# Writing the input gates' rows straight to their partitions, with new slot tables: an xLSTM, attention and expert kernel on one core

## What is computed

```python
igate = gate_input @ ig_kernel + ig_bias         # (8, 512, 4)
fgate = gate_input @ fg_kernel + fg_bias
cums = cumsum(log_sigmoid(fg))                   # F
log_D = cums[t] - cums[s] + ig[s]                # t >= s, else -inf
D = exp(log_D - max_log_D)                       # max over s
C = (q k^T / sqrt(64)) * D
h = (C / (max(|sum C|, exp(-max_log_D)) + eps)) @ v
x = x + headnorm(h)
...
q, k, v = per mixture m and head, of layernorm(x)
attn = softmax(q k^T / 4)                        # 2 x 16 heads, 512 x 512 per batch
x = x + sum_m probs_m * (attn v) wo_m
x = x + sum over the best 2 experts of p_k * (gelu(n2 fw1_k) fw2_k)
```

## Time and profile before

| | |
|---|---|
| median of 3 runs | 1423.28 us (1422.08 to 1424.86) |
| profiled execution | 1428.74 us |
| its span | 1426.9 us |
| PE busy | 1393.6 us, 98% |
| DVE, ACT, POOL busy | 77%, 64%, 25% |
| mean granted clock of PE | 0.99 of full speed |

### The profile page before, as it was taken

One profiled execution on the slowest core, in us unless ns is written; L12 is line 12 of the kernel. 1 busy time (PEld: TensorE's weight loads), 2 busy tenths in 40 slices (PEclk: granted clock), 3 DMA queues, 4 the chain that ended last, 5 costly groups with the idle time before them and its releaser, 6 DMA issues.

```text
span 1426.9 us, 22218 instructions
## 1 busy us (share of the span) xinstructions
PE 1393.6 (98%) x7666; PEld 716.9 (50%) x7666; DVE 1092.2 (77%) x2299; ACT 916.4 (64%) x1706; POOL 363.6 (25%) x351
## 2 busy tenths in 40 slices
PE   8999899999999999999999999999999999999999
PEld 5643434455454654555445554455545454454456
DVE  5779977987789877987779877797769986786721
ACT  3266557766677666675677765876666766757752
POOL 6512342203313123132241133130331322330000
PEclk9999999999999999999999999999999999999999
DMA  4056037430854127441464308541084413561002
GB/s 116 17 70 95 2 45 107 71 62 16 104 76 76 45 38 112 75 75 31 51 101 69 64 31 101 79 75 46 24 102 70 78 56 45 73 77 46 17 1 89
DMA packets 92308, 90.15 MB, mean 63 GB/s; under 512 B 16483, under 2 KB 87267, under 8 KB 91295
## 3 DMA queue, kind: packets, MB, share of 16 engines
q1 hardware_dynamic: 92196, 88.73, 38.6%
HBM read 35.05 MB, written 4.25 MB: 28 GB/s over the span
## 4 chain that ended last, share of the span: by engine, by line
PE 69%; issue 8%; DVE 4%; DMA 3%; SPq 2%; POOL 1%; ACT 1%; DVEq 0%; POOLq 0%; ACTq 0%
PE psum L881 12%; PE psum L866 12%; PE psum L851 12%; PE psum L819 7%; PE psum L838 6%; PE psum L701 5%; PE psum L452 5%; PE psum L736 3%; DMA qst<-mrow 3%; PE psum L475 2%; SPq L1954 2%; PE psum L563 2%; DVE mx L1378 1%; PE psum L573 1%; DVE x L1293 1%
## 5 line engine op out<-in xcount | busy, mean ns | idle before, releaser
L1378 DVE TENSOR_REDUCE mx<-psum 128x1 f32<-128x512 f32 x1024 | 645.5, 681 | 134.2 <-PE psum L851 133.5
L1677 ACT ACTIVATE prob<-psum 128x512 f32<-128x512 f32 x1024 | 568.2, 600 | 270.8 <-PE psum L881 159.4
L866 PE MATMUL psum<-qst,kst 98*128 98x512 bf16 x1024 | 355.9, 383 | 10.5 <-DMA qst<-mrow 8.7
L851 PE MATMUL psum<-kst,qst 96*128 96x512 bf16 x1024 | 318.8, 381 | 2.9 <-DVE resid L1252 1.3
L881 PE MATMUL psum<-prob,vst 128*17 128x512 f32 x2048 | 248.1, 601 | 2.7 <-ACT prob L1677 2.3
L866 PEld LDWEIGHTS psum<-qst,kst 98*128 98x128 bf16 x1024 | 96.9, 99 | 220.8 <-issue 126.9
L851 PEld LDWEIGHTS psum<-kst,qst 96*128 96x128 bf16 x1024 | 99.0, 98 | 121.2 <-issue 17.9
L881 PEld LDWEIGHTS psum<-prob,vst 128*17 128x17 f32 x2048 | 46.7, 97 | 136.3 <-issue 106.8
L838 PE MATMUL psum<-w,cxT 128*128 128x256 f32 x448 | 105.4, 381 | 0.0
L819 PE MATMUL psum<-n2T,x 128*128 128x512 f32 x224 | 103.0, 592 | 0.0
L1828 POOL CAST parts<-resid 128x512 bf16<-128x512 f32 x64 | 41.0, 640 | 239.9 <-DVE resid L1252 239.9
(11 more groups left out here) (244 smaller groups left out, 1761.5 us busy)
## 6 DMA issues: line engine op xcount, KB each, us to landing
kst<-parts SPq DMA_DIRECT2D x186, 128.0 KB, 4.7
qst<-parts SPq DMA_DIRECT2D x186, 128.0 KB, 5.9
cmat<-G_dram SPq DMA_DIRECT2D x7, 1024.0 KB, 4.6
x<-in_L_ffn_fw SPq DMA_DIRECT2D x14, 512.0 KB, 3.7
w<-in_L_ffn_fw SPq DMA_DIRECT2D x14, 512.0 KB, 4.2
xbuf<-in_x SPq DMA_DIRECT2D x8, 512.0 KB, 5.1
kin<-in_ctx SPq DMA_DIRECT2D x8, 512.0 KB, 4.5
out<-acc SPq DMA_DIRECT2D x7, 512.0 KB, 9.0
```

Source lines behind the costliest of these rows:

```text
L851: e.matmul(psum[:, u.bank, :], qst[0:KROWS, h, t * P:(t + 1) * P], kst[0:KROWS, h, :], start=True, stop=True).then_inc(u.full, 1)
L866: e.matmul(psum[:, u.bank, :], kst[0:KROWS + 2, h, g * P:(g + 1) * P], qst[0:KROWS + 2, h, :], start=True, stop=True).then_inc(u.full, 1)
L1378: e.tensor_reduce(mx[:, qq * QUAD + j, t:t + 1], psum[:, u.bank, :], AX, ALU.max).then_inc(u.free, 1)
L1677: e.activation(prob[:, g % 2, j, :], psum[:, u.bank, :], ACT.Exp).then_inc(u.free, 1)
```

## The change

ScalarE writes the input gates of PSUM rows 32 to 35 to partitions 0 to 3 of `cmat` itself. The eight transfers of SyncE go, and VectorE's step g waits for ScalarE's release of the PSUM bank. `load_x(1)` waits for the statistics of batch 0, which that transfer's place had covered. All slot tables and the `AHEAD` strings are new; three numbers that place steps beside them are too (`SENT` 0: `send_rows` stands one slot nearer to its maxima in SyncE's program; `MADE` 125 for 118: GpSimd's making of the expert input `x3`, L1875 and L1879, stands seven slots later; `COPY` 2 for 3). The diff, with SyncE's part of the `MIDDLE` table standing for all tables:

```diff
@@ -158,7 +158,6 @@
         gi, gf, ga, lf = (cmat[0:NH, r, :] for r in range(4))
-        gi_made = cmat[GI:GI + NH, 0, :]
@@ -290,86 +289,86 @@
-        CARRY, MADE = 9, 118
-        VALUES, COPY, TURN = 1, 3, 7
-        LATER, SENT = 1, 1
+        CARRY, MADE = 9, 125
+        VALUES, COPY, TURN = 1, 2, 7
+        LATER, SENT = 1, 0
...
         MIDDLE = dict(
...
-            SP_A=slots(5, "ctx:0 x:9 gi G:65 s0:16 s1:2 s2:23 s3"),
-            SP_C=slots(47, "w10:5 w20:9 w11:10 w21:30 out"),
-            SP_S=slots(7, "s4:5 s5:15 s6:15 s7"),
+            SP_A=slots(3, "ctx:2 x:16 G:65 s0:7 s1:22 s2:0 s3"),
+            SP_C=slots(47, "w10:8 w20:11 w11:6 w21:34 out"),
+            SP_S=slots(6, "s4:0 s5:19 s6:9 s7"),
...
@@ -990,7 +989,7 @@
                 yield "g"
-                e.wait_ge(gi_moved, 16 * (b + 1))
+                e.wait_ge(uses["gates", b].free, uses["gates", b].n)
                 e.wait_ge(*va.at("F", b))
                 e.tensor_tensor(rows[:, 0, :], gi, gf, ALU.subtract).then_inc(va.here("g", b), 1)
@@ -1495,7 +1494,7 @@
                 yield "grow0"
-                e.activation(gi_made, psum[GI:GI + NH, u.bank, :], ACT.Identity, bias=gbias[GI:GI + NH, :]).then_inc(u.free, 1)
+                e.activation(gi, psum[GI:GI + NH, u.bank, :], ACT.Identity, bias=gbias[GI:GI + NH, :]).then_inc(u.free, 1)
@@ -1962,6 +1961,8 @@
             def load_x(b):
+                if b == 1:
+                    e.wait_ge(*va.at("stat", 0))
                 if b > 2:
                     e.wait_ge(*pc.at("acc0", b - 3))
@@ -1973,10 +1974,6 @@
                 yield "x"
                 if b > 1:
                     load_x(b)
-                yield "gi"
-                u = uses["gates", b]
-                e.wait_ge(u.free, u.n)
-                e.dma_start(gi, gi_made).then_inc(gi_moved, 16)
                 yield "G"
```

More of the change, by code:

```diff
@@ L311, in build @@
[L311 to L321, removed]
@@ new lines, in build @@
+            ACT_C={},
+            ACT_S=slots(0, "p3:0 pv0:3 pv1:2 p4:2 p5:12 p6:2 p7:7 v0:16 v1"),
+            POOL_A=slots(-8, "pw:17 vcopy:19 mask0:12 mask1:0 mask2:26 mask3:4 vw:0 hw:5 hs:16 hn:15 x2:4 r1:0 r5 s0:5 "
+                         "s1:5 s2:2 s3"),
+            POOL_C={},
+            POOL_S=slots(7, "s3:10 s4:6 s5:15 s6:16 s7"),
+            SP_A=slots(-8, "ctx:4 x:24 G:53 s0:15 s1:20 s2:11 s3"),
+            SP_C={},
+            SP_S=slots(2, "s3:5 s4:10 s5:14 s6:22 s7"),
+            AHEAD="4043031012001321221113202113314000011203110030410000001310101001"
+                  "0211021003000002000033020200221102300110120123000011020102000000")
@@ L351, in build @@
         LAST = dict(
             PE_A={},
-            PE_C=slots(5, "cxT00:3 cxT01:2 cxT10 cxT11:2 wo0 wo1 wo2:3 wo3:22 mean:7 n2T0:0 n2T1:3 logits:9 hid00 "
-                       "hid01:0 hid02:0 hid03 eo00:8 eo01 eo02:6 eo03:2 hid10:51 hid11:2 hid12:0 hid13:0 eo10:2 "
-                       "eo11:0 eo12:0 eo13"),
-            PE_S=slots(5, "p4:2 p5:15 p6:2 p7:5 v0:8 v1"),
+            PE_C=slots(5, "cxT00:2 cxT01:3 cxT10:2 cxT11:2 wo0:8 wo1:4 wo2:2 wo3 mean:18 n2T0:0 n2T1:6 logits:7 "
+                       "hid00:0 hid01:0 hid02:2 hid03:2 eo00:0 eo01:5 eo02:8 eo03 hid10:51 hid11:2 hid12:0 hid13:0 "
+                       "eo10:2 eo11:0 eo12:0 eo13"),
@@ L357, in build @@
+            PE_S=slots(3, "p4:0 p5:18 p6:3 p7:6 v0:0 v1"),
             DVE_A={},
-            DVE_C=slots(13, "wo0 wo1 wo2:3 wo3:4 bn0 bn1:0 bn2:6 bn3:0 var:9 n20:5 n21:0 n22:0 n23:5 mean:2 logits "
-                        "topk:11 acc00:6 acc01:5 acc02:4 acc03:56 acc10:0 acc11:0 acc12:0 acc13"),
-            DVE_S=slots(5, "s4:4 s5:14 s6 s7"),
+            DVE_C=slots(14, "wo0:8 wo1:4 wo2:2 wo3:3 bn0:0 bn1:0 bn2:0 bn3:0 var:8 n20:0 n21:0 n22:0 n23:10 mean:2 "
+                        "logits:3 topk:9 acc00:4 acc01:2 acc02:5 acc03:59 acc10:0 acc11:0 acc12:0 acc13"),
@@ L365, in build @@
             POOL_A={},
-            POOL_C=slots(7, "acc0:47 r1"),
-            POOL_S=slots(5, "s4:0 s5:10 s6:13 s7"),
+            POOL_C=slots(27, "acc0:32 r1"),
+            POOL_S=slots(6, "s4:4 s5:10 s6:25 s7"),
             SP_A={},
-            SP_C=slots(47, "w10:10 w20:11 w11:16 w21:51 out"),
-            SP_S=slots(12, "s4:2 s5:14 s6:9 s7"),
-            AHEAD="4102131020121223412100210103000310113001021000030102110000341104"
-                  "0100313000310031212400100220120001120001203102000021210000101000")
+            SP_C=slots(43, "w10:0 w20:17 w11:21 w21:53 out"),
@@ L373, in build @@
+            SP_S=slots(3, "s4:17 s5:9 s6:0 s7"),
+            AHEAD="4141011211011111301212140140114010110020001210111120001104101313"
+                  "0200031010100041213020002120111002111104120000120000200100002020")
         for plan in (FIRST, MIDDLE, LAST):
```

69 lines of the change are left out of this document (35 added, 34 removed), and 12 rows, old and new, of the table DVE_A.

## The result

The changed kernel takes 1431.83 us (1431.05 to 1432.18, 5 runs) against 1423.28 (1422.08 to 1426.18, 5 runs): 1.0056 times as long, 95% interval 1.0043 to 1.0069, or 8 us slower. The forecast was 1419.6 and faster.

What follows compares the result with a forecast made beforehand. PE was taken as the bound, busy 1393.6 of 1426.9 us. 1.1 us (head) plus 2.6 us (slot 96) made 3.7 us off the 1423.28 us median, giving 1419.6 us, range 1415.0 to 1427.

Steps and rivals of the forecast that it cites:

- The head: Before the first period: without the gates' transfer, step g starts 1.09 us earlier; 1.1 us gain counted in full.
- Slot 96: Middle periods: two more scores and maxima before PE's wait for the row transfer shorten it by 0.44 us, six times: 2.6 us.
- Slot 0: Middle periods' end: send for next quad 0, queued behind s2, store and s3, taken as in time; bound 4 us loss.
- Period 0: Batch 0's period: its 2.93 us wait at slot 96 stays, other waits move by tenths; nothing counted, 1 us either way.
- A wait for `mx` or `prob` where more maxima stand together: Sign of being wrong: a new PE wait for these in slots where more maxima now stand together; no size given.
- The middle periods apart from slot 96: Six middle periods: slot 96 taken as each one's only wait, PE work staying at 166.1 us; nothing else counted.
- everything else equal: Middle periods, p0 to slot 96: PE's work changes only from 14 scores and maxima to 16.
- The last period: Last period: expert weight loads stand in other slots; nothing counted, one wait of 0.95 us kept as the bound.
- The sum against one profile: Whole kernel: 3.7 us taken off the median; batch 3's extra 2.6 us could explain half the profile's 5.46 us excess.
- only the head moves: Rival: slot-96 waits stay, giving 1422.2 us; chance 0.31, shared with a gain partly eaten by slot 0.
- the first score of a period waits: Slower rival: at a period's end the send for quad 0 lands late, 1.8 us six times, giving 1430.4; chance 0.17.
- the larger gain: Rival: period 0's new order makes up for its 2.93 us wait and no half clock follows, giving 1415.0; chance 0.09.

Runs made afterwards that it cites:

- e1: Kernel before with all its tables and numbers, only the direct write added (no transfer of the gates): 1421.57 us, 0.9996 of before.
- e3: Changed kernel with period 0's whole table (FIRST) of before: 1427.01 us, 1.0029 of before.
- e8: Changed kernel, period 0's five maxima of slots 58 to 65 moved to slots 68, 70 and 71: 1431.55 us, 1.0060 of before.
- e13b: Changed kernel with period 0's GpSimd and SyncE rows of before: 1432.22 us, 1.0054 of before.
- e0: The kernel before, unedited, profiled a second time: 1423.44 us, span 1421.6.
- e2: Changed kernel with the middle periods' whole table of before: 1430.33 us, 1.0051 of before.
- e5: Changed kernel, middle table: VectorE's variance in slot 3 instead of 5, third and fourth query normalisations in slot 9 instead of 6: 1440.72 us, 1.0126 of before.
- e9: Changed kernel, middle table: eight transpositions of the attention's output on TensorE and ScalarE in slot 10 instead of 12: 1440.01 us, 1.0119 of before.
- e12b: Changed kernel, middle table: VectorE's statistics in slot 2, variance in 3, normalisations in 5, instead of 3, 5 and 6: 1433.60 us, 1.0069 of before.
- e16: Changed kernel, middle table: maxima of the first 16 slots placed as before: 1440.17 us, 1.0116 of before.
- e6: Changed kernel, last table: VectorE's four normalisations (L1292) in slot 43 instead of 39: 1432.55 us, 1.0061 of before.
- e14b: Changed kernel, last table: VectorE's four normalisations (L1292) in slot 42 instead of 39: 1432.33 us, 1.0061 of before.
- e7: Changed kernel with the edits of e5 and e6, and period 0's normaliser in slot 63 instead of 60: 1440.75 us, 1.0114 of before.
- e10: Changed kernel with the edit of e9 and the first and last tables of before: 1434.63 us, 1.0078 of before.

## Why the prediction was wrong

The sum was 1.1 for the head and 2.6 for slot 96; the result was a loss of 8. The step that failed is the one that put the rest of the new tables at nothing: period 0, the last period, and the middle periods apart from slot 96. Before's table alone gave back 3.8, 1.1 and 0.7 us there.

- **The head, 1.1 us.** The mechanism was right: e1 and the changed kernel's head show it. The size came from an execution whose transfer was issued late; in the second profile the wait is 0.46 us at step g and 0.60 at PE, and e1 wins 0.6 us of head. The 1.4 us by which the two shown profiles differ at L660 is not what the median saw.
- **Slot 96, 2.6 us.** The mechanism was right, the size somewhat too large. In the changed kernel the waits of L865 on the row transfers are 5.7 us; without period 0's 3.3 the other six hold 2.4 us, where the six at slot 96 held 4.2. So 1.8 us came of the 2.6. Five of the six shrank by 0.3 to 0.55 us, as worked out; the one in batch 3's period grew from 0.62 to 0.95. It is 0.94 to 1.52 us in every profile with the new middle table, edited or not, and 0.52 to 0.92 with the old one. Why is open.
- **Slot 0, counted at nothing with a bound of 4 us.** Right in value; no wait. The queue's end was put 2 to 3.5 us too late, 1.8 of it because I kept quad 7's send at its old time.
- **Period 0, "nothing counted, 1 us either way kept".** The largest single part of what failed. With the old table, 3.8 us come back (e3). I compared its order only at p0 and slot 96. PE's idle time there rises from 9.5 to 10.6 us over the old table's profiles to 11.6 to 12.2, and its clock column from 1.7 or 3.4 us to 3.4 to 6.8, mostly 5.1. As its cause, e8 and e13b exclude five maxima of slots 58 to 65 and the order of GpSimd and SyncE. The most conspicuous new row is a wait of 1.43 us for ScalarE's `prob`, behind a load of its tables (1.28 us), but it is not the loss. With the old table PE waits as long near there, under other names. The changed kernel, then e3:

```profile
99.32 0.28 PE L451 MATMUL psum<-ident,mx 128*16 128x128 f32 x1 [1.43 <-ACT prob L1676]
```

```profile
95.97 0.38 PE L851 MATMUL psum<-kst,qst 96*128 96x512 bf16 x1 [1.27 <-DVE resid L1252]
...
104.39 0.39 PE L866 MATMUL psum<-qst,kst 98*128 98x512 bf16 x1 [0.64 <-DMA qst<-mrow]
```

With a wait of 0.66 us at 95.6 in the changed kernel that is 2.1 against 1.9 us, and the seventeenth score starts at 104.52 against 104.39. The new idle time is elsewhere: 1.0 us in the next eight slots (four waits of 0.2 to 0.4 us between 106 and 114 us, three of them for maxima), 1.0 us between slots 64 and 72 (4.1 against 3.1 in e0 and e1), and 0.3 us at slot 96 (3.29 against 2.93 to 2.98). A wait for `mx` or `prob` where more maxima stand together was on the prediction's list of signs of being wrong; it had no price there. Which moves cause these waits stays open.
- **The middle periods apart from slot 96, counted at nothing.** I said that "everything else equal" holds between p0 and slot 96, and looked at no other place. VectorE's normalisations had moved from slots 6 and 9 to slot 6 alone, and their variance from slot 3 to 5, and PE's cover from slot 10 to 12. That makes six new waits of 1.17 us, 7.0 us. Net it costs 0.7 us by the ratios (e2) or 1.5 by the medians, which is within the intervals, and 2.9 us in the profiles. That VectorE's normalisations take up to three times as long beside GpSimd is shown by their durations; that this alone makes them late is not. Four edits (e5, e9, e12b, e16) each left a wait of 1.3 to 1.9 us at or near the same place, in three of them under another name, and e5, e9 and e16 made the kernel slower by 8 to 9 us. The second table shows what that is: 5 us more idle time in each, and in e5 and e9 3.4 to 5.1 us of clock besides. What would cure it stays open.
- **The last period, counted at nothing with a bound of 0.95.** The old table gives 2.5 us back in the profile (193.8 to 191.3), in the ratio 1.1 with an interval that holds zero. The new wait of 1.38 us stands behind a VectorE group that took 3.52 us beside GpSimd's addition. e6 and e14b moved it off the collision and another wait of 0.9 to 1.0 us took its place, so its price is not shown by undoing it.
- **The sum against one profile.** 5.46 us lay between the profiled execution and the median. I called the 2.6 us of batch 3 possibly its own and left the rest. The second profile shows that the head's half-clock stretch was the other part: its head is 3.7 us shorter and batch 3's period 2.4. The changed kernel's span of 1429.6 is an ordinary one; set beside 1421.6, the difference is 8.0, as in the medians.

The rivals: that only the head moves, and that the first score of a period waits, are both excluded by the rows above, and the larger gain by the wait at slot 96 of period 0, which grew. The result fell on the slower side for none of the rivals' reasons. What I did not have among them was the plain one, that tables in which every engine's slots are new create new waits at places nobody looked at.

## What to carry to other kernels

When a change renumbers whole schedules, its named edit is a small part of it: compare each engine's position against its consumer's at every dependency, not only at the waits that exist now, since most of the waits that cost here are where there was none. In this kernel four tries to reorder VectorE's or PE's work around a wait of 1.2 us left one of 1.3 to 1.9 us; a wait's name is not its cause. And profile the same kernel twice before taking a sum from it: stretches at half clock come and go from one execution to the next and are as large as the gains looked for.

## What the runs showed that I had not expected

- In these profiles PE's granted clock is 1.00 (2.4 GHz) but for stretches at 0.50 (1.2 GHz) of 3.4 us or of twice that, 1.7 or 3.4 us each in the account. The kernel before has 13.6 us of it in one execution (6.8 + 3.4 + 1.7 + 1.7) and 5.1 in the next (1.7 + 3.4), with the same program. They lie near PE's longer waits (2.93 us at 200 us, 0.95 at 657), but not at each: e1 has the waits at 163 to 168 us that the kernel before has at 167 to 173, and no stretch there.
- In the middle periods the stretches went with the size of the wait near slot 10. Of 24 waits of 1.84 to 1.89 us (e5, e7, e9, e10), 13 had a stretch at half clock beginning within 1.1 us behind them; of 66 waits of 1.15 to 1.32 us there (eleven other profiles), one had, 2.0 us behind.
- VectorE's form of 128x256 f32 with one tensor input took 0.4 us alone and up to 1.3 us beside GpSimd's 1.16 us of L1829, and 2.5 us beside its 2.37 us of L1878. It then ends 0.14 to 0.15 us behind GpSimd's instruction in each case, so its length follows from when the other ends. The maxima read from PSUM took 0.65 to 0.69 us, alone or beside GpSimd.
- A larger wait row can cost little: 7.0 us of new waits in the middle periods made them 2.9 us longer than those of e2 (1005.5 against 1002.6), and 1.6 longer than those of e1 (1003.9), which hold a wait of 1.39 us of their own, for a row transfer.
